# Second attention: the last eight heads' scores go straight into ScalarE's exponential, and the values get a third buffer

## The chip, the cores and the metric

One Trainium2 chip, one of its cores. The time is device microseconds of one execution, median of the runs shown. The engines of a core run side by side, each in its own order, and wait for one another on semaphores: TensorE (PE, its weight loads PEld), VectorE (DVE), ScalarE (ACT), GpSimd (POOL), SyncE (SP, which issues DMAs).

## The reference, cut to what matters

The program is two layers of cross attention and mixture of experts over 4096 tokens of width 128 (64 rows of 64 tokens). The change lies in the attention of the second layer:

```python
qh = (q @ Wq + bq).reshape(b, lq, H, HD).transpose(0, 2, 1, 3)    # H = 16 heads of HD = 8
kh = (kv @ Wk + bk).reshape(b, lkv, H, HD).transpose(0, 2, 1, 3)
vh = (kv @ Wv + bv).reshape(b, lkv, H, HD).transpose(0, 2, 1, 3)
scores = jnp.einsum('bhqd,bhkd->bhqk', qh, kh) * scale[0]
attn = jax.nn.softmax(scores, axis=-1)
out = jnp.einsum('bhqk,bhkd->bhqd', attn, vh)
return out.transpose(0, 2, 1, 3).reshape(b, lq, DQ) @ Wo + bo
```

Each of the 64 rows attends to its own 64 context tokens. The softmax takes an extreme score off before the exponential. The kernel computes the scores with their sign turned, so it is the lowest one, and the exponent is lowest minus score.

## The kernel before, in words

The tokens are 32 tiles of 128 (two rows of 64). The function `combination_and_second_attention` has one instruction stream for each engine, written out as a march over slots, and nothing but that written order and the semaphores sets when a thing runs. The march is a software pipeline. I call **pass g** the slot in which VectorE takes the lowest scores of tile g. In pass g:

- **TensorE**: the scores of tile g in two halves of eight heads (L1815, into `pss[0]` and `pss[1]`; the first half waits for both differences of tile g-1, the second for the last exponential of tile g-1, which reads `pss[1]`); the projections of queries and keys of tile g+2 and of values of tile g (L1825 to L1831, into `psx`); `attend` for tile g-2 (L1863, L1868, into `pso`); every fourth pass the rank products of the router (L1875, L1876); `project` for tile g-3 (L1882); `turn`, the transposes of the exponentials of tile g-1 (L1890).
- **VectorE**: lowest score of the first half (L2168), difference (L2177, 128x512), lowest score of the second half, difference of heads 8 to 11 (L2177, 128x256), statistics (L2213), then `normalise` of tile g-2 (L2219 and L2221, which wait for `attend` and for `project` of this pass), `add_result` (L2239) and, depending on g modulo 4, a piece of the second router.
- **ScalarE**: the exponential of the first half (L1961); keys, queries and values out of `psx` (L1981, L1982, L1987; the values wait for `attend` of tile g-2 in this same pass, since tile g's values take its buffer); the second half: heads 12 to 15 each for itself straight from PSUM with the lowest score as the bias (L1964, four of 128x64), then heads 8 to 11 from VectorE's difference (L1966); in two passes of four the router's rows (L1970); then the transposed exponentials of tile g-1 out of PSUM (L2014), for which `attend` in the next pass waits.
- **GpSimd**: the blocked keys (L1742) and the indirect DMAs of the router (L1760). After the last tile it still has a row of these DMAs to issue, and the stage ends with them.

Ahead of the march the same streams clear tiles and weigh and sum the first layer's expert outputs. GpSimd clears the two value buffers `vb` (L1701) before it writes the index rows that VectorE waits for (L2061).

The router's work makes the passes unequal, with a period of four: passes 21, 25, ... choose the second expert, 22, 26, ... place the ranks, 23, 27, ... only take means, 24, 28, ... choose the first expert.

Of the kernel before, what the change touches and what calls it, by code (L numbers as in the profile page):

```python
# [11 lines left out]
ALU = mybir.AluOpType  # L12
# [3 lines left out]
P = 128  # L16
# [1540 lines left out]
def combination_and_second_attention(nc, C, A, G):  # L1557
# [8 lines left out]
    HG = 4  # L1566
    NP = H1 // 2
    NB = 3
    with ExitStack() as ctx:
        def two(name, shape, dt=F32):  # L1570
            return [C.sb(f"a1_{name}{j}", shape, dt, ctx=ctx) for j in range(2)]
# [7 lines left out]

        vb = two("vb", [P, 2 * NP * 32])  # L1580
        qt, kr, kb = two("qt", [P, P]), two("kr", [P, P]), two("kb", [P, 2, HG, T])
        mx, dd, pp = two("mx", [P, H1]), two("dd", [P, H1, T]), two("pp", [P, H1, T])
        pt = two("pt", [P, NP, P])
# [86 lines left out]
        with nc.Block(no_gpsimd_drain=True) as block:  # L1670
# [18 lines left out]
            def _(pool):  # L1689
# [9 lines left out]
                pool.sem_inc(s["zero"], 1)  # L1699
                for j in range(2):  # L1700
                    step.then(pool.memset(vb[j][:], 0.0))  # L1701
# [75 lines left out]
            def _(pe):  # L1777
# [25 lines left out]
                def slot_of(x):  # L1803
                    a, g, c, d = x.by(3), x.by(1), x.by(-1), x.by(-2)
                    if g.real():
                        pe.wait_ge(s["q_sb"], g.t + 1)
                        pe.wait_ge(s["kb"], g.t + 1)
                        after(pe, s["centred"], 2 * g.t)
                        for half in range(2):
                            if half == 1:  # L1810
                                after(pe, s["exp"], 2 * g.t)
                            for b in range(2):
                                for h in range(2):
                                    rows = slice(64 * half + 32 * h, 64 * half + 32 * h + 32)
                                    mm = pe.matmul(pss[half][T * b:T * b + T, h, 0:HG * T], qt[g.j][rows, T * b:T * b + T],  # L1815
                                                   kb[g.j][rows, b, :, :], start=True, stop=True)
                            mm.then_inc(s["scores"], 1)
# [37 lines left out]
                def attend(c):  # L1855
# [3 lines left out]
                    for b in range(2):  # L1859
                        for odd in range(2):  # L1860
                            for i in range(4):
                                k = 2 * i + odd
                                mm = pe.matmul(out[32 * i:32 * i + 32, T * b:T * b + T],  # L1863
                                               vb[c.j][:, 32 * (NP * b + k):32 * (NP * b + k) + 32],
                                               pt[c.j][:, k, T * b:T * b + T], start=odd == 0, stop=odd == 1)
# [35 lines left out]
                turn(t3)  # L1901
                pe.wait_ge(s["centred"], 2 * NT)
                project(t1)
# [27 lines left out]
            def _(act):  # L1931
# [23 lines left out]
                def exp(g, half):  # L1955
                    if g.real():
                        act.wait_ge(s["centred"], 2 * g.t + half + 1)
                        after(act, s["turned"], 2 * (g.t - 2) + half + 1)
                        h = slice(8 * half, 8 * half + 8)
                        if half == 0:  # L1960
                            act.activation(pp[g.j][:, h, :], dd[g.j][:, h, :], ACT.Exp).then_inc(s["exp"], 1)  # L1961
                        else:
                            for k in range(HG):
                                act.activation(pp[g.j][:, 12 + k, :], pss[1][:, 1, k * T:(k + 1) * T], ACT.Exp,  # L1964
                                               scale=-1.0, bias=mx[g.j][:, 12 + k:13 + k])
                            act.activation(pp[g.j][:, 8:12, :], dd[g.j][:, 8:12, :], ACT.Exp).then_inc(s["exp"], 1)  # L1966

# [5 lines left out]
                def slot_of(x):  # L1973
# [9 lines left out]
                    if g.real():  # L1983
                        after(act, s["o"], g.t - 1)
                        for odd in range(2):
                            v = psx[T * odd:T * odd + T, 256:384].rearrange("p (k c d) -> p k c d", c=2, d=DH1)
                            m = act.activation(vb_rows(g.j, odd), v, ACT.Copy)  # L1987
                        m.then_inc(s["v_sb"], 1)
# [59 lines left out]
            def _(dve):  # L2048
# [110 lines left out]
                def slot_of(x):  # L2159
# [9 lines left out]

                    def centre(half):  # L2170
                        groups = 2 - half
                        heads = slice(8 * half, 8 * half + HG * groups)
                        m = mx[g.j][:, heads].rearrange("p (g h) -> p g h", g=groups)
                        out = dd[g.j][:, heads, :].rearrange("p (g h) k -> p g h k", g=groups)
                        dve.wait_ge(s["lowest"], 2 * g.t + half + 1)
                        after(dve, s["exp"], 2 * (g.t - 2) + half + 1)
                        TT(out, wide(m.unsqueeze(3), [P, groups, HG, T]), scores(half)[:, 0:groups], ALU.subtract).then_inc(s["centred"], 1)  # L2177

                    if g.real():
                        after(dve, s["exp"], 2 * (g.t - 1))  # L2180
                        for half in range(2):
                            highest(half)
                            centre(half)
                    if n.real():
# [400 lines left out]
```

## Time and profile before

| | us |
|---|---|
| median of 3 runs | 937.81 |
| lowest, highest | 936.6, 942.0 |
| the profiled execution | 936.64 |
| its span | 935.4 |
| of it, tiles of the second attention, from the first lowest score to the last exponential | 576.2 to 765.1 |
| TensorE, VectorE, ScalarE, GpSimd busy over the span | 710.3, 673.2, 473.4, 564.8 |

The mean granted clock of TensorE was 0.799 of full speed. The steady part of the march takes 23.9 us for four tiles: VectorE takes the first lowest score of tile 21 at 700.39 us and that of tile 25 at 724.29. To see what sets this number, one has to go from engine to engine along the waits of a few passes, which the rows further down allow. An engine's busy share over the span says little, because the program has many stages with different limits.

### The profile page before, as it was taken

The page shows a single profiled execution, that of the slowest core. Times are in us where ns is not written, and L with a number is a line of the kernel's source. Part 1 is how long each engine was busy: PE and PEld are TensorE (multiplying, and loading weights), DVE is VectorE, ACT ScalarE, POOL GpSimd, SP SyncE. Part 2 cuts the span into 40 slices and gives each one's busy share as a digit, 9 for nine tenths or more (in the row PEclk, how much of TensorE's full clock was granted, in tenths as well). Part 3 has the DMA queues.
Part 4 walks back from the last instruction along what each step waited for, and adds up shares of the span by engine and source line. Part 5 has one row for each costly group of instructions (what it writes and reads, how often), then busy time and mean ns, then how long its engine had stood idle before and what let it go on. Part 6 is the DMA issues. An engine that isn't in the chain of part 4 may idle for free. (4 is left out here: it accounts for less than half of the span.)

```text
span 935.4 us, 20537 instructions
## 1 busy us (share of the span) xinstructions
PE 710.3 (76%) x6072; PEld 508.4 (54%) x6072; DVE 673.2 (72%) x3212; ACT 473.4 (51%) x1318; POOL 564.8 (60%) x931
## 2 busy tenths in 40 slices
PE   0686898979883999972498528998888874799970
PEld 0353554545483656631275426766666652699970
DVE  6898989978524688769111167598998887699974
ACT  3566576735200455450133175577777761577740
POOL 7688877766526544210677667345777767277770
PEclk9767787957555999996599855798988885899995
DMA  6300112997213977700365330000000002698928
GB/s 143 57 25 10 41 45 64 86 88 96 40 45 140 290 250 257 243 23 0 39 115 132 88 137 1 2 4 13 25 26 25 25 28 76 216 279 264 260 69 270
DMA packets 98829, 94.41 MB, mean 101 GB/s; under 512 B 37511, under 2 KB 82302, under 8 KB 98142
## 3 DMA queue, kind: packets, MB, share of 16 engines
q1 hardware_dynamic: 91268, 79.34, 33.1%
q0 software_dynamic: 6592, 13.58, 6.0%
q8 instruction: 50, 0.82, 0.4%
q14 instruction: 61, 0.50, 0.3%
q10 hardware_dynamic: 858, 0.17, 0.1%
HBM read 47.76 MB, written 43.19 MB: 97 GB/s over the span
## 5 line engine op out<-in xcount | busy, mean ns | idle before, releaser
L2402 POOL DMA_INDIRECT expert_pairs<-e_ys,e_home x78 | 75.4, 967 | 38.4 <-issue 23.5
L1742 POOL TENSOR_SCALAR a_kb<-a_kr,a_m,a_bk 128x128 f32<-128x128 f32 x128 | 57.9, 452 | 44.4 <-ACT a_kr L1981 32.3
L1760 POOL DMA_INDIRECT expert_slots<-r_rows,r_slotu x64 | 63.3, 989 | 30.3 <-DVE r_rows L2136 15.1
L950 DVE MATCH_REPLACE8 work<-m,work 128x64 f32<-128x64 f32 x384 | 75.7, 207 | 0.0
L1484 POOL DMA_INDIRECT ex_rows<-rows,slot_source x32 | 30.7, 960 | 52.7 <-POOLq L1163 43.2
L937 DVE MAX8 m<-work 128x8 f32<-128x64 f32 x384 | 57.0, 209 | 0.0
L825 PE MATMUL psf<-filmw,us 97*128 97x512 f32 x64 | 51.6, 902 | 3.0 <-ACT FO L846 2.9
L1815 PE MATMUL a_pss<-a_kb,a_qt 32*64 32x256 f32 x512 | 41.5, 463 | 13.9 <-ACT a_pp L1966 11.7
L2168 DVE TENSOR_REDUCE a_mx<-a_pss 128x8 f32<-128x512 f32 x64 | 43.9, 686 | 8.1 <-PE a_pss L1815 7.8
L2369 PE MATMUL e_ps<-e_XH,e_wh 128*128 128x256 f32 x156 | 48.1, 308 | 1.5 <-DVE e_XL L2414 1.5
L1536 ACT ACTIVATE ex_hs<-ex_psh,vec 128x512 f32<-128x512 f32 x32 | 22.0, 687 | 51.2 <-PE ex_psh L1517 50.5
L2371 PE MATMUL e_ps<-e_XH,e_wl 128*128 128x256 f32 x156 | 44.6, 286 | 0.0
L2370 PE MATMUL e_ps<-e_XL,e_wh 128*128 128x256 f32 x156 | 44.6, 286 | 0.0
L1961 ACT ACTIVATE a_pp<-a_dd 128x512 f32<-128x512 f32 x32 | 20.2, 631 | 45.1 <-DVE a_dd L2177 45.1
L1890 PE MATMUL a_psp<-ident,a_pp 128*128 128x128 f32 x256 | 39.5, 306 | 1.9 <-ACT a_pt L2014 1.9
L2219 DVE RECIPROCAL a_rt<-a_pso 128x128 f32<-128x128 f32 x31 | 29.5, 951 | 14.8 <-PE a_pso L1882 11.9
L1309 ACT ACTIVATE rt_rs<-mlp_psh,vec 128x512 f32<-128x512 f32 x32 | 22.0, 687 | 34.7 <-PE mlp_psh L1267 34.7
L203 POOL TENSOR_SCALAR mlp_ln_v<-mlp_ln_mv 128x4 f32<-128x4 f32 x24 | 5.5, 229 | 54.0 <-DVE mlp_ln_mv L195 54.0
L1494 POOL DMA_INDIRECT planes<-ex_ys,slot_home x32 | 31.2, 976 | 10.9 <-issue 9.1
L2177 DVE TENSOR_TENSOR a_dd<-a_mx,a_pss 128x512 f32<-128x512 f32 x64 | 35.5, 554 | 2.2
L808 PE MATMUL pss<-kb,qt 128*64 128x256 f32 x128 | 28.9, 541 | 10.7 <-ACT kb L846 10.7
L2014 ACT ACTIVATE a_pt<-a_psp 128x512 f32<-128x512 f32 x64 | 35.4, 611 | 2.2 <-PE a_psp L1890 2.0
(464 smaller groups left out, 2418.2 us busy)
## 6 DMA issues: line engine op xcount, KB each, us to landing
expert_slots<-rt_unfilled SPq DMA_DIRECT2D x151, 130.0 KB, 2.6
ahead<-folded_weights SPq DMA_DIRECT2D x20, 386.0 KB
e_wf<-folded_weights SPq DMA_DIRECT2D x19, 386.0 KB, 4.2
planes<-rt_zeros SPq DMA_DIRECT2D x4, 1024.0 KB
ew<-in_L_ffn_ew SPq DMA_DIRECT2D x16, 256.0 KB, 4.0
pair_y<-expert_pairs SPq DMA_DIRECT2D x16, 256.0 KB, 5.6
e_xr<-expert_slots SPq DMA_DIRECT2D x27, 130.0 KB, 3.3
folded_weights<-fold_done SPq DMA_DIRECT2D x8, 384.0 KB, 4.3
```

Source lines behind the costliest of these rows:

```text
L825: pe.matmul(psf[:], us[j][:], G.filmw[:], start=True, stop=True).then_inc(s["film"], 1)
L937: mx = dve.max(m8[x.j][:, h, r, :], src[:, h, :])
L950: return own.did(dve.match_replace(wk_[x.j][:, h, :], m8[x.j][:, h, r, :], src[:, h, :], TAKEN))
L1742: m = pool.tensor_scalar(kb[a.j][:, :, h, :], k, m4[:, h:h + 1], bk4[:, h:h + 1], ALU.mult, ALU.add)
L1760: pool.indirect_dma_start(G.slots, bass.IndirectOffsetOnAxis(ap=slot[:, b, k, t:t + 1], axis=0), rb[b % NB][:, k, t, :], None).then_inc(se ...
L1815: mm = pe.matmul(pss[half][T * b:T * b + T, h, 0:HG * T], qt[g.j][rows, T * b:T * b + T], kb[g.j][rows, b, :, :], start=True, stop=True)
L1890: mm = pe.transpose(psp[half][:, k, :], pp[x.j][:, h:h + 2, :].rearrange("p h k -> p (h k)"), G.ident[:])
L2168: dve.tensor_reduce(m, scores(half), AX.X, ALU.min).then_inc(s["lowest"], 1)
L2369: pe.matmul(psh[m][c][:], wh[j][:, m, c, :], XH[j][:], start=True, stop=False)
L2370: pe.matmul(psh[m][c][:], wh[j][:, m, c, :], XL[j][:], start=False, stop=False)
L2371: pe.matmul(psh[m][c][:], wl[j][:, m, c, :], XH[j][:], start=False, stop=True).then_inc(h_ps[m][c], 1)
L2402: pool.indirect_dma_start(G.pair, bass.IndirectOffsetOnAxis(ap=home[i % NY][:, k:k + 1], axis=0), ys[i % NY][:, k, :], None).then_inc(kept ...
```

## The change

Heads 8 to 11 are now treated as heads 12 to 15 were: no difference on VectorE, and ScalarE's exponential reads their scores in PSUM, with scale -1 and the lowest score as the bias. So tile g's second half is eight activations of 128x64. The difference tile `dd` shrinks to eight heads, `centred` counts once per tile, and ScalarE waits for `lowest` in place of `centred`. TensorE waits for the first half's difference alone before it writes the next tile's first scores. The values get three buffers in place of two, so that copying tile g's values waits for `attend` of tile g-3, a pass earlier, and GpSimd clears three.

```diff
+        NV = 3
+        vb = [C.sb(f"a1_vb{j}", [P, 2 * NP * 32], ctx=ctx) for j in range(NV)]
-        mx, dd, pp = two("mx", [P, H1]), two("dd", [P, H1, T]), two("pp", [P, H1, T])
+        mx, dd, pp = two("mx", [P, H1]), two("dd", [P, H1 // 2, T]), two("pp", [P, H1, T])
...
-                for j in range(2):
+                for j in range(NV):
                     step.then(pool.memset(vb[j][:], 0.0))
...
-                        after(pe, s["centred"], 2 * g.t)
+                        after(pe, s["centred"], g.t)
...
                         else:
-                            for k in range(HG):
-                                act.activation(pp[g.j][:, 12 + k, :], pss[1][:, 1, k * T:(k + 1) * T], ACT.Exp,
-                                               scale=-1.0, bias=mx[g.j][:, 12 + k:13 + k])
-                            act.activation(pp[g.j][:, 8:12, :], dd[g.j][:, 8:12, :], ACT.Exp).then_inc(s["exp"], 1)
+                            act.wait_ge(s["lowest"], 2 * g.t + 2)
+                            for k in range(8):
+                                m = act.activation(pp[g.j][:, 8 + k, :], pss[1][:, k // HG, k % HG * T:(k % HG + 1) * T], ACT.Exp,
+                                                   scale=-1.0, bias=mx[g.j][:, 8 + k:9 + k])
+                            m.then_inc(s["exp"], 1)
...
-                        after(act, s["o"], g.t - 1)
+                        after(act, s["o"], g.t - NV + 1)
...
                     if g.real():
                         after(dve, s["exp"], 2 * (g.t - 1))
-                        for half in range(2):
-                            highest(half)
-                            centre(half)
+                        highest(0)
+                        centre()
+                        highest(1)
```

ScalarE in two passes of the march, before, from the values to the transposed exponentials. `a_vb` are the values, `a_pp` the exponentials, `a_dd` the differences, `a_pss` the scores, `a_mx` the lowest scores, `a_pt` the transposed exponentials:

```order
L1987 ACTIVATE a_vb<-a_psx 64x8x2x8 x2
L1964 ACTIVATE a_pp<-a_pss,a_mx 128x64 x4
L1966 ACTIVATE a_pp<-a_dd 128x256
L1970 ACTIVATE r_rows<-X,r_shift,r_rstd 128x2x128 x2
L2008 ACTIVATE r_rows<-r_home 128x8
L2014 ACTIVATE a_pt<-a_psp 128x512 x2
```

and the same place now:

```order
L1988 ACTIVATE a_vb<-a_psx 64x8x2x8 x2
L1965 ACTIVATE a_pp<-a_pss,a_mx 128x64 x8
L1971 ACTIVATE r_rows<-X,r_shift,r_rstd 128x2x128 x2
L2009 ACTIVATE r_rows<-r_home 128x8
L2015 ACTIVATE a_pt<-a_psp 128x512 x2
```

One activation of 256 columns has become four of 64, and all that follows on ScalarE stands behind them as before.

VectorE from the lowest scores to the normalised output of the tile two before (`a_rt`, `a_of`), before:

```order
L2168 TENSOR_REDUCE a_mx<-a_pss 128x8
L2177 TENSOR_TENSOR a_dd<-a_mx,a_pss 128x512
L2168 TENSOR_REDUCE a_mx<-a_pss 128x8
L2177 TENSOR_TENSOR a_dd<-a_mx,a_pss 128x256
L2213 BN_STATS r_st<-X 128x6
L2219 RECIPROCAL a_rt<-a_pso 128x128
L2221 TENSOR_TENSOR a_of<-a_pso,a_rt 128x128
```

and now:

```order
L2169 TENSOR_REDUCE a_mx<-a_pss 128x8
L2175 TENSOR_TENSOR a_dd<-a_mx,a_pss 128x512
L2169 TENSOR_REDUCE a_mx<-a_pss 128x8
L2212 BN_STATS r_st<-X 128x6
L2218 RECIPROCAL a_rt<-a_pso 128x128
L2220 TENSOR_TENSOR a_of<-a_pso,a_rt 128x128
```

The difference of 256 columns has left the row between the second lowest score and the statistics. Nothing else changed its place.

## Rows read from the trace of the kernel before

**Rows 1.** Windows: the march, a stretch of low clock, one of high clock

```profile
core 0: us, PE busy (x) PEld busy (x) DVE busy (x) ACT busy (x) POOL busy (x), PEclk, DMA share, GB/s
577.00:762.00 185.00, 165.87 (x2650) 119.39 (x2652) 154.36 (x445) 131.54 (x404) 115.15 (x193) 0.84 0.05 17
706.50:713.00 6.50, 6.03 (x78) 4.82 (x78) 5.23 (x17) 4.42 (x14) 4.83 (x9) 0.50 0.07 23
713.50:730.00 16.50, 14.38 (x266) 10.03 (x267) 15.16 (x44) 12.88 (x40) 13.14 (x20) 1.00 0.07 23
```

**Rows 2.** Waits, 577 to 766: total us, times, longest

```profile
ACT a_pp L1961 <- DVE a_dd L2177: 45.1, 32, 2.2
...
DVE a_rt L2219 <- PE a_pso L1882: 11.9, 16, 1.4
...
ACT a_vb L1987 <- PE a_pso L1868: 5.5, 7, 2.8
```

**Rows 3.** Timeline, passes 21 and 22: start, us, engine, line

```profile
700.39 0.69 DVE L2168 TENSOR_REDUCE a_mx<-a_pss 128x8 f32<-128x512 f32 x1
...
701.83 0.63 ACT L1961 ACTIVATE a_pp<-a_dd 128x512 f32<-128x512 f32 x1 [1.29 <-DVE a_dd L2177]
...
703.44 0.93 ACT L1964 ACTIVATE a_pp<-a_pss,a_mx 128x64 f32<-128x64 f32 x4
...
704.24 0.43 ACT L1966 ACTIVATE a_pp<-a_dd 128x256 f32<-128x256 f32 x1
...
704.55 1.10 ACT L1970 ACTIVATE r_rows<-X,r_shift,r_rstd 128x256 f32<-128x256 f32 x2
...
704.73 0.66 PE L1815 MATMUL a_pss<-a_kb,a_qt 32*64 32x256 f32 x8 [0.95 <-ACT a_pp L1966]
...
705.63 1.09 ACT L2014 ACTIVATE a_pt<-a_psp 128x512 f32<-128x512 f32 x2
...
706.97 1.08 PE L1863 MATMUL a_pso<-a_pt,a_vb 128*32 128x64 f32 x32 [0.56 <-ACT a_pt L2014]
...
709.71 0.80 PE L1882 MATMUL a_pso<-a_wo,a_of 128*128 128x136 f32 x2
...
710.62 0.96 DVE L2219 RECIPROCAL a_rt<-a_pso 128x128 f32<-128x128 f32 x1 [1.06 <-PE a_pso L1882]
...
713.58 0.69 DVE L2168 TENSOR_REDUCE a_mx<-a_pss 128x8 f32<-128x512 f32 x1
```

**Rows 4.** Timeline, passes 23 and 24, to the start of pass 25

```profile
717.44 0.43 ACT L1966 ACTIVATE a_pp<-a_dd 128x256 f32<-128x256 f32 x1
...
717.92 0.66 PE L1815 MATMUL a_pss<-a_kb,a_qt 32*64 32x256 f32 x8 [0.68 <-ACT a_pp L1966]
...
719.53 0.65 PE L1863 MATMUL a_pso<-a_pt,a_vb 128*32 128x64 f32 x32
...
720.55 0.50 PE L1882 MATMUL a_pso<-a_wo,a_of 128*128 128x136 f32 x2
...
721.16 0.96 DVE L2219 RECIPROCAL a_rt<-a_pso 128x128 f32<-128x128 f32 x1 [0.54 <-PE a_pso L1882]
...
724.29 0.69 DVE L2168 TENSOR_REDUCE a_mx<-a_pss 128x8 f32<-128x512 f32 x1
```

**Rows 5.** Groups by line and shape, VectorE, 577 to 765: busy, mean ns | idle before

```profile
L2177 DVE TENSOR_TENSOR a_dd<-a_mx,a_pss 128x256 f32<-128x256 f32 x32 | 13.5, 422 | 1.1
```

**Rows 6.** The same for ScalarE

```profile
L1964 ACT ACTIVATE a_pp<-a_pss,a_mx 128x64 f32<-128x64 f32 x128 | 29.8, 315 | 0.8
...
L1966 ACT ACTIVATE a_pp<-a_dd 128x256 f32<-128x256 f32 x32 | 13.8, 432 | 0.0
```

**Rows 7.** Timeline ahead of the march, and its first tiles

```profile
536.54 1.11 POOL L1701 MEMSET a_vb<- 128x512 f32 x2 [0.15 <-POOL a_m L1697]
...
539.00 0.18 DVE L2061 CAST r_tile_f<-r_tile_i 128x39 f32<-128x39 int32 x1 [1.90 <-POOL r_tile_i L1708]
...
540.07 0.28 ACT L1937 ACTIVATE comb_cstt<-a_pss 128x128 f32<-128x128 f32 x1 [5.15 <-PE a_pss L1782]
...
580.50 1.13 PE L1815 MATMUL a_pss<-a_kb,a_qt 32*64 32x256 f32 x8 [0.59 <-ACT a_pp L1966]
```

**Rows 8.** Timeline, the end of the march on GpSimd

```profile
765.31 0.24 POOL L1725 TENSOR_SCALAR r_v<-r_mv 128x4 f32<-128x4 f32 x1 [0.95 <-DVE r_mv L2190]
```

**Rows 9.** Timeline, from pass 11 to pass 12, where the clock fell

```profile
645.72 0.43 ACT L1966 ACTIVATE a_pp<-a_dd 128x256 f32<-128x256 f32 x1
...
650.18 0.96 DVE L2219 RECIPROCAL a_rt<-a_pso 128x128 f32<-128x128 f32 x1 [1.35 <-PE a_pso L1882]
```

**Rows 10.** Windows, columns as in rows 1, within pass 12

```profile
648.50:651.50 3.00, 3.00 (x26) 2.50 (x18) 1.61 (x6) 2.33 (x9) 2.45 (x4) 0.50 0.09 28
```

More of the change, by code:

```diff
@@ L1578, in combination_and_second_attention @@
         ones = C.sb("a1_ones", [P, 2, 2, 2, DH1], ctx=ctx)
-        vb = two("vb", [P, 2 * NP * 32])
+        NV = 3
+        vb = [C.sb(f"a1_vb{j}", [P, 2 * NP * 32], ctx=ctx) for j in range(NV)]
         qt, kr, kb = two("qt", [P, P]), two("kr", [P, P]), two("kb", [P, 2, HG, T])
-        mx, dd, pp = two("mx", [P, H1]), two("dd", [P, H1, T]), two("pp", [P, H1, T])
+        mx, dd, pp = two("mx", [P, H1]), two("dd", [P, H1 // 2, T]), two("pp", [P, H1, T])
         pt = two("pt", [P, NP, P])
@@ L1863, in attend @@
                                 mm = pe.matmul(out[32 * i:32 * i + 32, T * b:T * b + T],
-                                               vb[c.j][:, 32 * (NP * b + k):32 * (NP * b + k) + 32],
+                                               vb[c.t % NV][:, 32 * (NP * b + k):32 * (NP * b + k) + 32],
                                                pt[c.j][:, k, T * b:T * b + T], start=odd == 0, stop=odd == 1)
@@ L1901, in _ @@
                 turn(t3)
-                pe.wait_ge(s["centred"], 2 * NT)
+                pe.wait_ge(s["centred"], NT)
                 project(t1)
@@ L1956, in exp @@
                     if g.real():
-                        act.wait_ge(s["centred"], 2 * g.t + half + 1)
                         after(act, s["turned"], 2 * (g.t - 2) + half + 1)
-                        h = slice(8 * half, 8 * half + 8)
                         if half == 0:
-                            act.activation(pp[g.j][:, h, :], dd[g.j][:, h, :], ACT.Exp).then_inc(s["exp"], 1)
-                        else:
-                            for k in range(HG):
-                                act.activation(pp[g.j][:, 12 + k, :], pss[1][:, 1, k * T:(k + 1) * T], ACT.Exp,
-                                               scale=-1.0, bias=mx[g.j][:, 12 + k:13 + k])
-                            act.activation(pp[g.j][:, 8:12, :], dd[g.j][:, 8:12, :], ACT.Exp).then_inc(s["exp"], 1)
+                            act.wait_ge(s["centred"], g.t + 1)
+                            act.activation(pp[g.j][:, 0:8, :], dd[g.j][:], ACT.Exp).then_inc(s["exp"], 1)
+                        else:
+                            act.wait_ge(s["lowest"], 2 * g.t + 2)
[3 more added lines that the diff above has]
+                            m.then_inc(s["exp"], 1)
                 def keep_rows(b, k):
@@ L1983, in slot_of @@
                     if g.real():
-                        after(act, s["o"], g.t - 1)
+                        after(act, s["o"], g.t - NV + 1)
                         for odd in range(2):
                             v = psx[T * odd:T * odd + T, 256:384].rearrange("p (k c d) -> p k c d", c=2, d=DH1)
-                            m = act.activation(vb_rows(g.j, odd), v, ACT.Copy)
+                            m = act.activation(vb_rows(g.t % NV, odd), v, ACT.Copy)
                         m.then_inc(s["v_sb"], 1)
@@ L2168, in highest, with centre @@
                         dve.tensor_reduce(m, scores(half), AX.X, ALU.min).then_inc(s["lowest"], 1)
[L2170 to L2177, printed above, removed]
+                    def centre():
+                        m = mx[g.j][:, 0:8].rearrange("p (g h) -> p g h", g=2)
+                        dve.wait_ge(s["lowest"], 2 * g.t + 1)
+                        after(dve, s["exp"], 2 * (g.t - 2) + 1)
+                        TT(dd[g.j][:].rearrange("p (g h) k -> p g h k", g=2), wide(m.unsqueeze(3), [P, 2, HG, T]), scores(0),
+                           ALU.subtract).then_inc(s["centred"], 1)
                     if g.real():
                         after(dve, s["exp"], 2 * (g.t - 1))
-                        for half in range(2):
-                            highest(half)
-                            centre(half)
+                        highest(0)
+                        centre()
+                        highest(1)
                     if n.real():
```

## The prediction

> **What bounds the kernel now.** I read the windows first, to see which engine is fullest in the stage that changes; then the waits, to see who is really waited for; then the timeline of four passes, to follow the waits round until they close into a loop. In the march VectorE is busy 154.4 of 185 us, ScalarE 131.5, GpSimd 115.2 [rows 1]. That alone would make VectorE the bound and the change a gain. The waits say otherwise: VectorE itself waits 16 times, 11.9 us in all, with the reciprocal, for TensorE's `project` [rows 2]. 16 is every second tile. So there is a loop that goes through VectorE in one place only, and it is two passes long.
>
> Follow it from the start of pass 21 [rows 3]. VectorE begins with the lowest score at 700.39. Lowest score and first difference take until ScalarE can start the first exponential at 701.83. ScalarE then copies keys, queries and values, starts the second half's exponentials at 703.44 and ends them at 704.24 + 0.43 = 704.67. Call that moment E: it is 4.28 after the pass began. TensorE has been idle for 0.95 us and starts the second scores of tile 22 at 704.73, released by E. ScalarE goes on with the router's rows (704.55) and the transposed exponentials (705.63 to 706.72), and `attend` starts behind these at 706.97, after 0.56 idle. `project` ends at 709.71 + 0.80 = 710.51, and VectorE, idle for 1.06 us, starts the reciprocal at 710.62. From E to there it is 5.95. The rest of pass 22 is VectorE alone: 2.96 us until it begins pass 23 at 713.58.
>
> The second loop of the period has the same form [rows 4]. Pass 23 begins at 713.58, E is at 717.44 + 0.43 = 717.87 (4.29 later), TensorE is released after 0.68 idle, and runs through scores, projections, `attend` and `project` to 721.05; the reciprocal, after 0.54 idle, starts at 721.16 (3.29 after E). 3.13 later pass 25 begins, at 724.29. The sum of both is 4.28 + 5.95 + 2.96 + 4.29 + 3.29 + 3.13 = 23.90, which is the measured 724.29 - 700.39. So these loops are the bound. The second lowest score and the second difference of pass 21 and 23 lie in neither of them: they run on VectorE while ScalarE does the first exponential and the copies. In passes 22 and 24 they run ahead of a reciprocal that waits anyway.
>
> **The change part by part.**
>
> *The second difference goes.* 32 of 422 ns, 13.5 us of VectorE [rows 5]. By the loops above, this is worth nothing as long as the reciprocal waits: it waits 1.06 and 0.54 now, and with 0.42 less ahead of it, it waits 1.48 and 0.96.
>
> *ScalarE's second half gets longer.* Four activations of 64 columns start at 703.44 and the next instruction at 704.24, so each takes 0.20 of the engine's time though it lasts 0.315 from end to end [rows 3, 6]. Now there are eight: the last starts at 703.44 + 7 x 0.20 = 704.84 and ends at 705.16. E was 704.67, so it comes 0.49 later. These are on both loops, with nothing beside them: TensorE waits for E, and the rows, the transposed exponentials and with them `attend` stand behind it on ScalarE. Passes 9, 11, ... 29 each start such a loop: 11 x 0.49 = **+5.4 us**. Could the activations cost less from PSUM bank to bank, or more? The four of before read the same kind of tile with the same kind of bias, so I take the row's value; the bounds are 0.10 (four new ones hidden but for a pipeline's worth) and 0.83 (four at 0.315 without overlap, less the 0.43 that goes).
>
> The Trainium skill, "ScalarE: Activation LUTs", section on what ACT_TABLE_LOAD costs, gives an activation with a per-partition bias 280 ns + 0.833 ns a column, one with immediates 186 ns + 0.833 ns a column, and an overlap of 93 ns back to back. By it four more would cost 4 x 240 and the one that goes 306 ns, so E would move by an estimated 0.65, and the term would be +7.2. The row shows 0.20 for each, not 0.24, and I go by the row.
>
> *The third value buffer.* The values' copy waited 7 times, 5.5 us in all, the longest 2.8 [rows 2]; these waits lie mostly in the first tiles. In the steady passes 21 and 23 the copy does not wait, so it gives the loops nothing. In the opening TensorE works without a stop at the low clock, and an earlier copy only makes ScalarE wait elsewhere. Passes 5 to 8 are light (no router work yet) and there the copy's wait was in E. Tiles 3 to 8 together: 2 x 0.49 more for the exponentials, about half of it paid back by that wait. I take **+0.45**, an estimate, between -1.0 and +1.0.
>
> *The first tile.* TensorE stood idle 0.59 until tile 0's last exponential let it write the second scores [rows 7], and from there it works without a stop for several tiles: **+0.49**.
>
> *The third clearing.* 1.11 / 2 = 0.56 us on GpSimd, ahead of the index row for which VectorE waits 1.90 until 539.00; behind that stand VectorE's sum, TensorE's transpose and ScalarE, idle 5.15 us until 540.07 [rows 7]. Nothing covers it: **+0.56**, between 0 and 0.6.
>
> *The end.* GpSimd starts its last row of work at 765.31, released by VectorE's statistics of pass 31 [rows 8]. There VectorE is the one waited for, and a difference less lies ahead: **-0.42**.
>
> *TensorE's earlier leave for the first scores* is worth nothing, for the second scores wait for E right behind them.
>
> Sum at an unchanged clock: 5.4 + 0.45 + 0.49 + 0.56 - 0.42 = **+6.5 us**.
>
> *The clock.* TensorE's clock is at its lower level (1.2 GHz, 0.50) from 706.5 to 713, at 1.00 from 713.5 to 730 [rows 1]; it fell after TensorE's idle times of 0.95 and 0.56 in passes 21 and 22, and did not fall after the 0.68 at 717.92. Both idle times now grow by about 0.5. The first loop is run at the low level already. The second would lose if the clock fell there too: at pass 12 it was low, and E to reciprocal took 650.18 - (645.72 + 0.43) = 4.03 in place of 3.29 [rows 9, 10], 0.74 more. I count this for half of the 5.5 second loops: **+2.0**, bounds -8 and +12 (below).
>
> The sum is +8.5. The profiled execution took 936.64, of it 935.4 in the span, so 945.1 for one like it; the median of the runs lies 1.2 above it, and by that I forecast 946.3.
>
> **The rivals.**
>
> *The saved VectorE time counts (faster).* If the loops are not what holds the passes, VectorE is, as the fullest engine. Without its waits of 1.60 the period is 22.3, and with 4 x 0.42 less it is 20.6. The mechanism would be that `project` comes early enough: it decides where E to reciprocal is under the 6.0 us or so that VectorE takes from E of one pass to the reciprocal of the next. Part of it would do: if VectorE's saving alone set the pace, 5.5 periods x 1.7 = -9.3, with +0.56 and +0.49 and -0.42: 929.1. For it speaks the share of 83%; against it stand the 16 waits. The Trainium skill, "Perfetto Trace Analysis", section on optimizing Scalar/DVE operations, says that work may be moved from DVE to Scalar where DVE is saturated; by that rule this rival is right, and the trace does not agree, for a saturated engine would not stand idle before every second reciprocal. 0.10.
>
> *The clock stays high in the first loop (no change).* At the low clock `attend`, ranks and `project` took 706.97 to 710.51, 3.54; at the high one `attend` and `project` took 719.53 to 721.05, 1.52 [rows 3, 4], and with the ranks, by estimate, 2.1. If passes of another length let the clock be high there, each period gains 1.4: 5.5 x 1.4 = -7.9 against +6.5, 936.4. For it: the clock's stretches come and go, and this one meets the same place every period. Against: the idle time that goes before it grows. 0.13.
>
> *The clock falls in every second loop (slower still).* Then 3.29 becomes, at the ratio of the two `attend` rows (1.08 to 0.65), up to 5.4 in each of 5.5 loops: +11.6 in place of +2.0, 955.9. 0.12.
>
> *Nothing that can be measured.* The added activations are hidden, and E moves by 0.10 only: +1.1 in place of +5.4, no clock term, 939.9. 0.07.
>
> **How the numbers follow.** Forecast 0.58 (941 to 951), faster through VectorE 0.10, high clock 0.13, low clock 0.12, hidden 0.07. Half a percent, 4.7 us, is about what a measurement of this kernel can tell from no change: faster means under 933.1, slower over 942.5. Faster: 0.10 + 0.02 of the high clock = 0.12. Same: 0.11 of the high clock, 0.07, and 0.05 of the forecast's lower end = 0.23. Slower: 0.65. The range leaves out the VectorE case and little else: 934 to 956.
>
> **What would show it.** In the profile after: E 4.78 after the start of passes 21 and 23 (eight activations 1.7 us from first start to last end); the reciprocal still waits in every second pass, longer, over 17 us in all; four tiles take 24.9 us or more; the wait of the values' copy is gone; VectorE is busy 13 us less in the march and idle more. I am wrong if the waits before the reciprocal vanish, if the four new activations take less than 0.20 each, or if the clock share of the march, 0.84, moves by more than 0.05.

## The result, and the profile after

The changed kernel is slower: 955.35 us median of 6 runs against 937.41 for the kernel before beside it, ratio 1.0195, 95% interval 1.0142 to 1.0248. Measured again later it took 945.2 (6 runs) against 936.03, ratio 1.0119, 1.0063 to 1.0176. The ratios here and below compare fast runs with fast ones, so they are not exactly the quotients of the medians beside them. Single executions spread widely here, those of the kernel before from 928 to 944 us on one chip, so ratios are to be read with their intervals, and single profiles by stage and not by their total.

The profiled execution took 948.62 us, its span 947.4, which is 12.0 more than before. The first lowest score of the march, that of the last tile, and the last indirect DMA of GpSimd cut this into pieces. 1.81 us had come before the stage began, in code that is the same: GpSimd clears its first tile of the stage at 536.08, not 534.27. (In the profiles of this study the first lowest score stands anywhere from 567.8 to 580.6 us.) 0.57 lie between the stage's start and the first lowest score. From there to the lowest score of tile 31 it is 193.59 in place of 185.11, 8.48 more. From there to GpSimd's last row of DMAs it is 0.19 less, and 1.33 more come behind the stage, again in unchanged code. So 8.9 of the 12.0 lie in the stage that the change touches.

Passes 21 and 22 of the changed kernel, in the timeline, as [rows 3] had them:

```profile
706.92 0.69 DVE L2169 TENSOR_REDUCE a_mx<-a_pss 128x8 f32<-128x512 f32 x1
...
708.43 0.64 ACT L1961 ACTIVATE a_pp<-a_dd 128x512 f32<-128x512 f32 x1 [2.17 <-DVE a_dd L2175]
...
710.04 1.75 ACT L1965 ACTIVATE a_pp<-a_pss,a_mx 128x64 f32<-128x64 f32 x8
...
711.84 1.12 PE L1816 MATMUL a_pss<-a_kb,a_qt 32*64 32x256 f32 x8 [1.92 <-ACT a_pp L1965]
...
714.67 1.08 PE L1864 MATMUL a_pso<-a_pt,a_vb 128*32 128x64 f32 x32
...
717.41 0.80 PE L1883 MATMUL a_pso<-a_wo,a_of 128*128 128x136 f32 x2
...
718.32 0.96 DVE L2218 RECIPROCAL a_rt<-a_pso 128x128 f32<-128x128 f32 x1 [2.95 <-PE a_pso L1883]
```

and passes 23 and 24, to the start of pass 25, as [rows 4]:

```profile
721.16 0.69 DVE L2169 TENSOR_REDUCE a_mx<-a_pss 128x8 f32<-128x512 f32 x1
...
724.27 1.75 ACT L1965 ACTIVATE a_pp<-a_pss,a_mx 128x64 f32<-128x64 f32 x8
...
726.08 0.66 PE L1816 MATMUL a_pss<-a_kb,a_qt 32*64 32x256 f32 x8 [0.61 <-ACT a_pp L1965]
...
729.32 0.96 DVE L2218 RECIPROCAL a_rt<-a_pso 128x128 f32<-128x128 f32 x1 [1.28 <-PE a_pso L1883]
...
732.52 0.69 DVE L2169 TENSOR_REDUCE a_mx<-a_pss 128x8 f32<-128x512 f32 x1
```

The same loops, longer. As in the prediction, **E** is the end of a pass's last exponential; the first loop of a period is passes 21 and 22, the second passes 23 and 24. Eight exponentials take 1.75 us from first start to last end, and E is at 711.79, 4.87 after the start of the pass (4.28 before). TensorE is idle for 1.92 until then, not 0.95. The reciprocal waits 2.95 and 1.28 us, not 1.06 and 0.54. The first loop takes 721.16 - 706.92 = 14.24 (13.19 before), the second 732.52 - 721.16 = 11.36 (10.71). Four tiles take 25.6 us.

The groups by line and shape show where VectorE's freed time went (busy, mean ns | idle before):

```profile
L2218 DVE RECIPROCAL a_rt<-a_pso 128x128 f32<-128x128 f32 x30 | 28.6, 954 | 36.3 <-PE a_pso L1883 34.7 <-PE a_pso L1869 1.6
```

```profile
L1965 ACT ACTIVATE a_pp<-a_pss,a_mx 128x64 f32<-128x64 f32 x256 | 56.0, 330 | 0.8
```

The reciprocal alone now stands behind 36.3 us of idle time; its wait for `project` was 11.9 [rows 2]. From the first lowest score to the last exponential VectorE is busy 146.4 us (576.1 to 765.1 before: 158.2), 11.9 less, and the march is longer. The wait of the values' copy, 5.5 us before, is gone. The windows of the changed kernel, the whole march, its opening and its steady part, with the granted clock as the number after the five engines:

```profile
578.50:776.50 198.00, 173.33 (x2677) 126.60 (x2674) 145.92 (x423) 149.51 (x509) 118.47 (x198) 0.81 0.05 16
578.50:630.00 51.50, 46.53 (x711) 33.48 (x708) 33.61 (x78) 38.79 (x135) 22.66 (x45) 0.86 0.01 2
630.00:776.50 146.50, 126.80 (x1966) 93.12 (x1966) 112.31 (x346) 110.71 (x374) 95.81 (x153) 0.79 0.07 21
```

The clock share of the march went from 0.84 [rows 1] to 0.81. In the steady part it is 0.79, where the kernel before had this:

```profile
629.40:765.00 135.60, 118.32 (x1957) 85.30 (x1945) 120.83 (x365) 98.77 (x305) 95.19 (x151) 0.86 0.07 23
```

### The profile page after: what moved, and what is told of

Its sections match the earlier page's. It is cut to its first block and busy times, and to the rows that moved or that the text cites. A ratio compares the mean times of both kernels' runs of the same rounds, so it can differ in the third digit from the quotient of the medians.

```text
span 947.4 us, 20572 instructions
## 1 busy us (share of the span) xinstructions
PE 716.0 (76%) x6072; PEld 516.2 (54%) x6072; DVE 661.3 (70%) x3180; ACT 489.1 (52%) x1414; POOL 565.2 (60%) x932
## 5 line engine op out<-in xcount | busy, mean ns | idle before, releaser
L1965 ACT ACTIVATE a_pp<-a_pss,a_mx 128x64 f32<-128x64 f32 x256 | 56.0, 330 | 0.8
L2218 DVE RECIPROCAL a_rt<-a_pso 128x128 f32<-128x128 f32 x31 | 29.6, 954 | 36.3 <-PE a_pso L1883 34.7
L1891 PE MATMUL a_psp<-ident,a_pp 128*128 128x128 f32 x256 | 41.5, 317 | 1.8 <-ACT a_pt L2015 1.8
L1309 ACT ACTIVATE rt_rs<-mlp_psh,vec 128x512 f32<-128x512 f32 x32 | 22.0, 687 | 34.7 <-PE mlp_psh L1267 34.7
L1891 PEld LDWEIGHTS a_psp<-ident,a_pp 128*128 128x128 f32 x256 | 37.2, 169 | 2.3 <-ACT a_pp L1965 2.0
```

What stands on the lines that cost most here:

```text
L1891: mm = pe.transpose(psp[half][:, k, :], pp[x.j][:, h:h + 2, :].rearrange("p h k -> p (h k)"), G.ident[:])
L1965: m = act.activation(pp[g.j][:, 8 + k, :], pss[1][:, k // HG, k % HG * T:(k % HG + 1) * T], ACT.Exp, scale=-1.0, bias=mx[g.j][:, 8 + k:9 + k])
```

## The experiments

The theory to be tested, called the loop theory: the pace is set by loops of two passes that run through ScalarE's E, TensorE's `attend` and `project`, and VectorE's reciprocal; VectorE's second difference lies in neither. The rivals: VectorE's time counts; every pass counts alike; the third value buffer costs; the loss is TensorE's clock.

A number is used below that is read alike from each profile: the start of the lowest score of tile 29 less that of tile 9, over five, the **period** for four tiles. It is 23.75 for the kernel before and 25.70 for the changed one. Each run was profiled once, and the clock makes the period vary: two more profiles of the changed kernel, the last with two waits in another order, have 26.64 and 25.91. So periods of one kernel can lie almost one us apart, and a smaller difference is only used with the single loops beside it.

### The parts apart

**The third value buffer alone**, in the kernel before:

```diff
-        vb = two("vb", [P, 2 * NP * 32])
+        NV = 3
+        vb = [C.sb(f"a1_vb{j}", [P, 2 * NP * 32], ctx=ctx) for j in range(NV)]
...
-                        after(act, s["o"], g.t - 1)
+                        after(act, s["o"], g.t - NV + 1)
```

> The kernel before with the third value buffer alone; scores and exponentials as before. The loop theory (the second half's last exponential, E, sets the pace of every second pass): four tiles still take 23.9 us in the steady part, 0.6 us more for the third clearing, up to 1 us less in the light passes 5 to 8, so 936 to 938.5. The rival that the third buffer itself costs (clearing, place in memory): 940 or more.

Measured: 937.88 against 937.06, ratio 1.0019, 0.9975 to 1.0063; period 23.92. The buffer neither costs nor brings anything that can be measured.

**The exponentials alone**, that is the changed kernel with two value buffers:

```diff
-        NV = 3
+        NV = 2
```

> The changed kernel with two value buffers, so the eight exponentials from PSUM alone. The loop theory: E comes 0.58 later after the start of passes 21 and 23 (4.87 against 4.29), four tiles take 25.6 us, and the whole loss is here: 950 to 957, like the changed kernel. If the two parts share the loss: about 946.

Measured: 948.01 against 937.06, ratio 1.0137, 1.0091 to 1.0183, just under the 950 to 957 expected. The loss is here. The period was only 24.41, though, not 25.6: E came 4.86 after the start of the pass as in the changed kernel, but in most of its first loops TensorE's clock was high, and E to reciprocal took 4.37 there. From pass 9 to 29 the clock was 0.93, in the kernel before 0.87. The second loop of pass 15, which ran at the high level throughout in both, took 11.34 us in place of 10.71 all the same: so the clock is not the whole of the loss. The values' copy waited again, 16 times, as this row of the waits says (total us, times, longest):

```profile
ACT a_vb L1988 <- PE a_pso L1869: 12.4, 16, 2.7
```

and in passes 27 and 29 this wait pushed E to 7.00 and 5.80 after the start. So with the longer exponentials the third buffer does take a wait out of a loop, which it did not in the kernel before. Whether it brings time on the whole the ratios (1.0137 without, 1.0195 and 1.0119 with it) don't tell.

### VectorE's time

**The changed kernel with a subtraction put back on VectorE**, of the same shape as the one taken out:

```diff
                         highest(0)
                         centre()
                         highest(1)
+                        spare()
```

`spare` subtracts 128x256 of the first difference from the lowest scores, into a tile that nothing reads.

> The changed kernel, with a subtraction of 128x256 put back on VectorE behind the second lowest score; its result is not used. The loop theory: VectorE's waits before the reciprocal shrink by the 0.4 us that is put in, the period stays at 25.6 and the time at the changed kernel's, 950 to 957. If VectorE's time counts, 32 x 0.42 come on top: 962 or more.

Measured: 949.47 against 937.06, ratio 1.0133, 1.0094 to 1.0173, which is no more than the changed kernel's 1.0195 and 1.0119, and far from the 962 of the rival. The run with the exponentials alone, on the same chip and without this work, took 948.01. Putting 13.5 us of work back on the fullest engine cost nothing that the runs can tell. The period of its one profile, 26.39, is not below the changed kernel's, and not clear of the 26.64 that the changed kernel's second profile had. The wait before the reciprocal became shorter instead, 28.4 us for `project` in the waits where the changed kernel had 34.7:

```profile
DVE a_rt L2229 <- PE a_pso L1884: 28.4, 15, 2.7
```

**The opposite of the change**: VectorE takes all eight differences of the second half, ScalarE does one exponential.

```diff
-                        groups = 2 - half
+                        groups = 2
...
-                        if half == 0:
-                            act.activation(pp[g.j][:, h, :], dd[g.j][:, h, :], ACT.Exp).then_inc(s["exp"], 1)
-                        else:
-                            for k in range(HG):
-                                act.activation(pp[g.j][:, 12 + k, :], pss[1][:, 1, k * T:(k + 1) * T], ACT.Exp,
-                                               scale=-1.0, bias=mx[g.j][:, 12 + k:13 + k])
-                            act.activation(pp[g.j][:, 8:12, :], dd[g.j][:, 8:12, :], ACT.Exp).then_inc(s["exp"], 1)
+                        act.activation(pp[g.j][:, h, :], dd[g.j][:, h, :], ACT.Exp).then_inc(s["exp"], 1)
```

> The kernel before, moved the other way: VectorE takes the difference of all eight heads of the second half (128x512) and ScalarE one exponential of 128x512 in place of five activations. The loop theory: E comes 0.6 earlier after the start of the pass, VectorE does 0.27 more in each; the first loop falls from 13.2 to 12.6, the second is then held by VectorE at 10.6, four tiles take 23.2, and the time is about 934. If VectorE sets the pace, 32 x 0.27 come on top: 946.

Measured: 935.21 against 937.06, ratio 0.9958, 0.9912 to 1.0004; period 23.24, the 23.2 that was worked out. More work on the fullest engine and a time that is not longer. Pass 21 of it, in the timeline:

```profile
697.25 0.69 DVE L2162 TENSOR_REDUCE a_mx<-a_pss 128x8 f32<-128x512 f32 x1
...
700.30 0.63 ACT L1960 ACTIVATE a_pp<-a_dd 128x512 f32<-128x512 f32 x1
```

E is 3.68 after the start. Here VectorE is the bound at last: from pass 9 to pass 29 its reciprocals wait 0.6 us in all, in the kernel before 6.9.

### Which passes count

The sharpest cut: the changed second half for the tiles of one parity only, in the kernel before (two value buffers). `differences(t)` counts VectorE's differences ahead of tile t. The even one:

```diff
-                        act.wait_ge(s["centred"], 2 * g.t + half + 1)
+                        straight = half == 1 and g.t % 2 == 0
+                        if straight:
+                            act.wait_ge(s["lowest"], 2 * g.t + 2)
+                        else:
+                            act.wait_ge(s["centred"], differences(g.t) + half + 1)
...
-                            for k in range(HG):
-                                act.activation(pp[g.j][:, 12 + k, :], pss[1][:, 1, k * T:(k + 1) * T], ACT.Exp,
-                                               scale=-1.0, bias=mx[g.j][:, 12 + k:13 + k])
-                            act.activation(pp[g.j][:, 8:12, :], dd[g.j][:, 8:12, :], ACT.Exp).then_inc(s["exp"], 1)
+                            for k in range(0 if straight else HG, 2 * HG):
+                                m = act.activation(pp[g.j][:, 8 + k, :], pss[1][:, k // HG, k % HG * T:(k % HG + 1) * T], ACT.Exp,
+                                                   scale=-1.0, bias=mx[g.j][:, 8 + k:9 + k])
+                            if not straight:
+                                m = act.activation(pp[g.j][:, 8:12, :], dd[g.j][:, 8:12, :], ACT.Exp)
+                            m.then_inc(s["exp"], 1)
...
-                            centre(half)
+                            if half == 0 or g.t % 2 != 0:
+                                centre(half)
```

> The kernel before, with the changed second half (eight exponentials from PSUM, no second difference) for the tiles of even number alone; two value buffers. The loop theory: the loops run through E of the odd passes alone, so 16 later E and 16 differences less change nothing: 23.9 us for four tiles, 935 to 939. If each pass counts alike (by ScalarE's time or by VectorE's), half of the loss or gain is seen: 942 or more, or 933 or less.

> The same for the tiles of odd number alone. The loop theory: all of the loss is here. E comes 0.5 to 0.6 later in passes 21 and 23, four tiles take 25 us or more, 945 to 950. If each pass counts alike: 942, as with the even tiles.

Measured: even tiles 941.76 against 938.15, ratio 1.0032, 0.9992 to 1.0072, period 23.87. Odd tiles 951.32 (4 runs), ratio 1.0134, 1.0059 to 1.0210, period 26.21. The edit is of the same size in both: 16 groups of eight exponentials, 16 differences less. The medians lie 9.6 us apart and the intervals of the ratios overlap a little. The even kernel's median is also close to the 942 of the rival by which each pass counts alike, but that rival wanted 942 for the odd one too.

The totals hide other things that differ, so the loops have to be looked at one by one. With odd tiles E comes 4.79 or 4.80 after the start of eight of the ten odd passes from 9 to 27, 0.5 later than in the kernel before. Pass 25 (start of the pass, the eight exponentials):

```profile
737.42 0.69 DVE L2177 TENSOR_REDUCE a_mx<-a_pss 128x8 f32<-128x512 f32 x1
...
740.48 1.74 ACT L1971 ACTIVATE a_pp<-a_pss,a_mx 128x64 f32<-128x64 f32 x8
```

In the other two, 11 and 23, the values' copy waited and E came at 5.9. With even tiles E stays at 4.28 in five of the ten (9, 15, 17, 21 and 27), and the second loops of passes 15 and 27 take 10.71, as before. In passes 11 and 23 E came at 5.16 and 6.58: the values' copy waited there for 0.76 and 1.26, and in pass 23 the keys' copy for 0.81.

So the even kernel's unchanged period is a sum of things that cancel: over the ten odd passes from 9 to 27, 4.1 us of later E, and 3.1 less from E to reciprocal at a clock of 0.91, not 0.87. With odd tiles the same stretch took 12.3 us more than before: 5.1 are the later exponentials, 2.1 the copy's waits, 3.7 lie between E and reciprocal, and 1.4 behind the reciprocal, with two delays of 1.1 that are described at the end. What parts the two kernels in every pass is the 0.5 by which the odd tiles' exponentials move E. That the time saved on VectorE in the even tiles brings nothing agrees with a total that is not shorter, but is not shown here apart from those tiles' later exponentials.

### The clock

**The changed kernel again**, for the size of the loss:

> The changed kernel again, unaltered, beside the others of this row on one chip, for a better size of the loss and of TensorE's clock. The loop theory with the clock: 950 to 955, mean granted clock about 0.01 under the kernel before. If the loss were the later exponentials alone, without the clock: 937 + 0.6 + 11 x 0.58 + 0.6, 945.

Measured: 945.2 against 936.03, ratio 1.0119, 1.0063 to 1.0176. This is under the 950 to 955 that were expected and is the 945 named for a loss without the clock. The profile doesn't bear that out: its period is 26.64, its march 198.25, which is 13.1 more than in the kernel before, and from E to the reciprocal four of the five second loops from pass 9 took 4.46 to 4.67 in place of 3.29. It is a short execution (941.6) because the code ahead of the march took 8.4 us less than in the kernel before. So neither the total nor one profile gives the clock's share.

**First scores of the even tiles computed twice**, to fill TensorE's idle time before E:

```diff
-                            for b in range(2):
-                                for h in range(2):
+                            for b, h in [(b, h) for _ in range(2 if half == 0 and g.t % 2 == 0 else 1) for b in range(2) for h in range(2)]:
```

> The changed kernel in which TensorE computes the first half's scores of every even tile twice, into the same place, before it reports them: the same result, and about 0.6 us of its idle time before the second scores filled. It tells the clock from the later exponentials. If idle time of TensorE is what lets the clock fall: the granted clock of the march rises from 0.81 to 0.85 or more, E to reciprocal in the first loop falls from 6.1 towards 5, and the time from 954 to 945 to 950 in spite of more work. If the clock has nothing to do with it: the same time or up to 3 us more.

Measured: 946.34 against 936.03, ratio 1.0123, 1.0076 to 1.0170, the time of the changed kernel beside it. It lies in the 945 to 950 expected, but those stood for a gain on a changed kernel of 954. Half of the expectation came: the granted clock of the march was 0.89 (0.81 and 0.84 in the two profiles of the changed kernel), E to reciprocal in the first loops 5.08 on average (6.13 and 6.04), and the period 24.89. But the whole did not become faster, against what was expected. With one profile of each, and totals that differ between executions by more than the effect, it stays open how much of the loss is the clock's: the rows show that E to reciprocal follows the clock, and the times don't show a gain from raising it this way.

### Mending the loops

If E and what stands between E and `attend` set the pace, ScalarE's order can be mended without any work moved. **The transposed exponentials ahead of the router's rows**, in the kernel before:

```diff
+                    if x.real():
+                        keep_turned(x)
                     if due(x, LG) is not None:
                         b = due(x, LG)
...
                         keep_places(b)
-                    if x.real():
-                        keep_turned(x)
```

> The kernel before, with ScalarE's copies of the transposed exponentials ahead of the router's rows in the two passes of four that have both. The loop theory: in pass 21 the rows (1.08 us) lie between E and what attend waits for; now attend waits for the projections instead, 0.55 earlier, the first loop falls from 13.2 to 12.6, the period from 23.9 to 23.4: 934. If those rows were hidden anyway, or something waits for them: 937 or more.

Measured: 935.25 against 936.03, ratio 0.9959, 0.9922 to 0.9996, period 23.54, a gain just clear of noise. **And the values' copy behind the exponentials**, in addition:

```diff
+                    if due(x, PLACE) is not None:
+                        second_gate(due(x, PLACE))
+                    exp(g, 1)
                     if g.real():
                         after(act, s["o"], g.t - 1)
                         for odd in range(2):
...
                         m.then_inc(s["v_sb"], 1)
-                    if due(x, PLACE) is not None:
-                        second_gate(due(x, PLACE))
-                    exp(g, 1)
```

> As the run before it, and the values are copied out of PSUM behind the second half's exponentials in place of ahead of them, so that E comes 0.57 earlier after the start of the pass (3.7). The loop theory: first loop 12.1, second 10.2, both now held by VectorE, which has 22.3 us of work in four passes: period 22.3, time 928. If the projections of the next pass wait for the values: the period stays at 23.4 or more, 934.

Measured: **927.7** against 936.03, ratio 0.9896, 0.9862 to 0.9930, period 22.51 (22.3 expected). This beats both kernels, by moving two steps on ScalarE. From pass 9 to pass 29 the reciprocals wait 1.5 us in all, in the kernel before 6.9. Pass 21:

```profile
695.61 0.69 DVE L2168 TENSOR_REDUCE a_mx<-a_pss 128x8 f32<-128x512 f32 x1
...
698.92 0.43 ACT L1966 ACTIVATE a_pp<-a_dd 128x256 f32<-128x256 f32 x1
699.80 1.08 ACT L2014 ACTIVATE a_pt<-a_psp 128x512 f32<-128x512 f32 x2
700.78 1.09 ACT L1970 ACTIVATE r_rows<-X,r_shift,r_rstd 128x256 f32<-128x256 f32 x2
```

E is 3.74 after the start, and the router's rows stand last. The same order in **the changed kernel**, the same moves:

> The changed kernel (three value buffers, eight exponentials) with ScalarE reordered as in the run with the values late: values behind the second half's exponentials, transposed exponentials ahead of the router's rows. The loop theory: E 4.3 after the start of the pass, loops 12.6 and 10.8, four tiles 23.4: 934 to 938, all of the loss won back, but not better than the kernel before by VectorE's 13.5 us, since the loops and not VectorE set the pace; slower than the reordered kernel before (928). If VectorE sets the pace once the order is mended: 20.5 for four tiles, 920.

Measured: 935.86 against 938.15, ratio 1.0001, 0.9955 to 1.0046. All of the loss is won back and nothing more, as the loop theory said; E is 4.28 after the start. Its profile had period 22.71, less than the 23.4 worked out; the clock was high in part of the first loops (E to reciprocal 3.84 to 5.59). The same order with the exponentials of before is a percent faster, so also here VectorE's saving doesn't pay for ScalarE's longer second half.

### A detail of the wait

The changed kernel, with ScalarE's wait for the difference ahead of the one for the transposes, as in the kernel before:

```diff
+                        if half == 0:
+                            act.wait_ge(s["centred"], g.t + 1)
                         after(act, s["turned"], 2 * (g.t - 2) + half + 1)
                         if half == 0:
-                            act.wait_ge(s["centred"], g.t + 1)
```

> The changed kernel with ScalarE's two waits ahead of the first exponential in the order of the kernel before (first for the difference, then for the transposes). For the trace alone: in the changed kernel the first exponential starts 0.09 after the difference ends, in the kernel before 0.03. If the order of the two waits makes that, it is 0.03 again and E comes 4.80 after the start of the pass in place of 4.86; if not, both stay.

Measured, in the trace: the first exponential starts 0.03 after the difference ends (0.09 in the changed kernel, 0.03 before), and E comes 4.80 after the start of the pass. Here it cost 0.06 that the wait which is met last also stood last. That is 0.06 of the 0.58 by which E moved. The kernel with the odd tiles alone, which has the waits in the order of before, agrees: E at 4.79. The one execution took 952.66, which says nothing of 0.06 in a pass.

## Why the prediction was right, and where it was off

The forecast was 946.3, range 934 to 956; measured 955.35 and, again, 945.2. The sign and the range held, and the mechanism in its main part. The range held narrowly: 955.35 is 9.0 above the forecast, 0.65 under the upper end, and next to the 955.9 of the rival by which the clock falls in every second loop.

- **What bounds the kernel: right.** The wait before every second reciprocal was read as a loop of two passes. The E of the odd tiles, the opposite of the change, which put more work on VectorE and was not slower, and the mended order of ScalarE show it.
- **The second difference is worth nothing: right.** The subtraction that was put back cost nothing measurable, and VectorE's busy time fell by 11.9 (13 forecast) while the march grew. Only at the stage's end was it counted as -0.42, and -0.19 came.
- **ScalarE's term was a bit small.** E moved by 0.58, not 0.49: 0.06 from the order of two waits that the change had swapped, which the prediction did not look at, and 0.03 from the eight activations themselves, 1.75 in place of 1.72. Eleven loops make 6.4 in place of 5.4. The spacing of the activations, (1.75 - 0.33) / 7 = 0.20, is the row's. The figures of the Trainium skill, "ScalarE: Activation LUTs", section on what ACT_TABLE_LOAD costs, give an estimated 0.24; the trace does not agree.
- **The third clearing: right**, 0.57 for 0.56.
- **The opening was wrong in sign.** Tile 0 and tiles 3 to 8 were to cost 0.49 and 0.45. From the first lowest score to that of tile 9 it took 51.42 us in place of 53.26, at a mean clock of 0.86 in place of 0.80. From tile 3 to tile 9 it was 33.46 in place of 32.74, 0.7 more for the 0.45 forecast; the error lies ahead of tile 3, 17.96 in place of 20.52. The changed kernel's second profile has 51.42 as well, at a clock of 0.90. The third buffer is not enough to explain it: the kernel with the two waits turned round has it too and took 55.75, at a clock of 0.78, the same buffer in the kernel before 54.02, also at 0.78, and the exponentials with two buffers 55.77, at 0.81. So in the changed kernel the piece was short where the clock was high; why the clock differs there stays open.
- **The clock term was right in kind and small in size.** From tile 9 to tile 29 the changed kernel took 128.52 us, 9.75 more. Ten loops with 0.58 are 5.8 of it. E to reciprocal gave 2.4 more in the first loops (5.95, 6.47, 5.94, 6.53, 5.94, where the kernel before had 5.31, 5.27, 5.95, 5.94, 5.95) and 2.2 more in the second (4.22, 3.29, 4.23, 3.29, 4.36, where it had 4.04 and four times 3.29); the pieces on VectorE gave 0.6 back. The forecast had 2.0 for both, all of it in the second loops, where 2.2 came: the clock fell in three of these five loops (in four in the second profile, with 4.46 to 4.67), not in each, and E to reciprocal never took the 5.4 that the rival allowed. The step that failed is "the first loop is run at the low level already", which put the first loops at nothing. Two of the five, those of passes 9 and 13, had not been, with 5.31 and 5.27, and that is 1.3 of the 2.4. Nor was 5.95 the end: 6.5 came when the scores were also done at the low level, at which the row of 1.12 us at 711.84 stands, and that is the other 1.1.
- **That the sum came out is in part luck.** The term for the march, the clearing and the end was 8.5 and came to 8.9 in the profiled execution, since the opening's error (-1.8 in place of +0.9) and those of the clock and of E cancel. In the second profile the march alone was 13.1 longer, 3.4 of it by the delays of the last section. The other 3 us of the first profile's 12 come from code that the change does not touch, and the two ratios, 1.0195 and 1.0119, differ by more than most of the terms above.

## What to carry to other kernels

Look for who waits for whom, and how often, before asking which engine is fullest: a wait at every second pass is a loop of two passes, and only work inside it counts. Before moving work from VectorE to ScalarE, find the instructions on ScalarE that others wait for, and what stands ahead of them: here moving the values' copy behind the exponentials and the router's rows behind the transposed exponentials brought 1.0%, and putting eight exponentials where there were five cost 1.2 to 2.0%. A small piece of work can be tested for worth by putting it into the even passes only, and the odd ones only; then compare the loops one by one, since the clock and other waits move the totals as well.

## What the runs showed of the hardware that was not expected

A scalar-tensor-tensor on VectorE, two inputs of 128x32 in SBUF, takes 0.19 to 0.25 us, 8 times in each kernel. In the changed kernel's second profile three of the eight took 1.31 or 1.32:

```profile
723.75 1.34 POOL L1734 TENSOR_TENSOR X<-X,e_cst 128x544 f32<-128x544 f32 x1
723.82 1.32 DVE L2106 SCALAR_TENSOR_TENSOR r_lg<-r_oh,r_lg 128x32 f32<-128x32 f32 x1
```

Each began 0.07 or 0.08 us after GpSimd had begun its addition of 1.34 us and ended 0.05 behind it. In the kernel before GpSimd's addition came later and the two did not meet:

```profile
700.14 0.21 DVE L2105 SCALAR_TENSOR_TENSOR r_lg<-r_oh,r_lg 128x32 f32<-128x32 f32 x1
...
701.77 1.34 POOL L1733 TENSOR_TENSOR X<-X,e_cst 128x544 f32<-128x544 f32 x1
```

That is 1.1 us in a second loop each time, since the next lowest score stands behind it; it was seen in one loop each of the kernels with the subtraction put back, with the scores twice and with the two waits turned round, and in two with the odd tiles alone. It was not tried by itself, but it makes up 3.4 of the 4.7 us by which the second profile's march is longer than the first's, and 0.4 of the odd tiles' period of 26.21. The Trainium skill, "SBUF — State Buffer", section on the rules for kernel authors, says that when VectorE has two SBUF inputs and GpSimd reads SBUF, the second to issue blocks until the first finishes; the trace agrees, 1.32 beside 1.34.
